# Top-2 experts on sorted rows: 23 padded tiles instead of all experts on all tokens

## The reference

```python
router_logits = xf @ router_w                      # (tokens, 8)
probs = softmax(router_logits)
rw, sel = top_k(probs, 2)
rw = rw / rw.sum(axis=-1, keepdims=True)
h = gelu(einsum('nc,ecf->enf', xf, w1e), approximate=False)   # 256 -> 512, each of 8 experts
y_all = einsum('enf,efc->nec', h, w2e)                        # 512 -> 256
y = (take_along_axis(y_all, sel) * rw[:, :, None]).sum(axis=1)
```

## Time and profile before

| | |
|---|---|
| median of 3 runs | 6225.56 us (6222.17 to 6227.89) |
| profiled execution, its time | 6224.38 us |
| profiled execution, its span | 6222.7 us |
| busy: PE, DVE, ACT, POOL | 4986.2, 4198.5, 2791.2, 1775.7 us |
| mean granted clock of TensorE | 0.88 |

### The profile page before, as it was taken

One profiled execution on the slowest core, in us unless ns is written; L12 is line 12 of the kernel. 1 busy time (PEld: TensorE's weight loads), 2 busy tenths in 40 slices (PEclk: granted clock), 3 DMA queues, 4 the chain that ended last, 5 costly groups with the idle time before them and its releaser, 6 DMA issues. The chain is left out here.

```text
span 6222.7 us, 84570 instructions
## 1 busy us (share of the span) xinstructions
PE 4986.2 (80%) x31689; PEld 3196.3 (51%) x31689; DVE 4198.5 (67%) x8611; ACT 2791.2 (45%) x5885; POOL 1775.7 (29%) x1429
## 2 busy tenths in 40 slices
PE   4444478888678988888678988889777998997789
PEld 2333345566335655666434654656534664665256
DVE  5999866777886856777786856668787755224511
ACT  2443315664354524656254633656344542553321
POOL 2565502333233401333232421334322430001000
PEclk7566689999789989999798998999888998998899
DMA  2000000000100110000201010000100010001000
GB/s 99 11 11 24 1 29 22 14 17 10 47 30 31 35 53 24 12 12 14 55 17 38 28 67 20 12 12 17 41 30 21 26 39 24 10 15 33 28 28 34
DMA packets 75086, 169.70 MB, mean 27 GB/s; under 512 B 15176, under 2 KB 36528, under 8 KB 71352
## 3 DMA queue, kind: packets, MB, share of 16 engines
q1 hardware_dynamic: 72632, 163.77, 8.3%
q10 hardware_dynamic: 2048, 0.53, 0.0%
HBM read 130.92 MB, written 26.26 MB: 25 GB/s over the span
## 5 line engine op out<-in xcount | busy, mean ns | idle before, releaser
L1373 DVE MAX8 vals<-work 128x8 f32<-128x128 f32 (+7 forms) x1536 | 1081.7, 745 | 0.6
L1718 POOL TENSOR_SCALAR keep<-ssb,vals 128x128 bf16<-128x128 f32 (+7 forms) x512 | 875.1, 1721 | 0.0
L1705 POOL TENSOR_TENSOR pool_step<-ones 128x2 f32<-128x2 f32 x256 | 49.5, 193 | 2536.4 <-DVE vals L1373 2536.2
L428 PE MATMUL ring<-ident,pr 128*128 128x128 f32 x2304 | 470.1, 323 | 360.4 <-POOL pr L1723 329.5
L1387 DVE MATCH_REPLACE8 work<-vals,work 128x128 f32<-128x128 f32 (+7 forms) x1024 | 751.5, 741 | 0.0
L535 PE MATMUL pA<-SC 128*128 128x512 f32 (+3 forms) x1536 | 626.7, 518 | 131.1 <-ACT SC L1116 109.6
L1723 POOL TENSOR_TENSOR pr<-keep,pr 128x128 f32<-128x128 bf16 (+7 forms) x512 | 647.2, 1285 | 0.0
L1055 ACT ACTIVATE prT<-ring 128x512 f32<-128x512 f32 (+1 forms) x768 | 379.4, 495 | 566.0 <-PE ring L428 564.8
L1502 DVE TENSOR_REDUCE nmax<-pA 128x1 f32<-128x1024 f32 (+7 forms) x512 | 382.7, 751 | 317.1 <-PE pA L536 306.0
L428 PEld LDWEIGHTS ring<-ident,pr 128*128 128x128 f32 x2304 | 326.4, 165 | 496.1 <-POOL pr L1723 355.3
L723 PE MATMUL pA<-hT,SC 128*128 128x512 f32 x1024 | 494.6, 606 | 0.0
(11 more groups left out here) (198 smaller groups left out, 8581.6 us busy)
## 6 DMA issues: line engine op xcount, KB each, us to landing
SC<-in_w SPq DMA_DIRECT2D x64, 512.0 KB, 4.4
parts<-SC SPq DMA_DIRECT2D x72, 256.0 KB, 2.4
SC<-in_wqkv SPq DMA_DIRECT2D x32, 384.0 KB, 2.9
stage<-parts SPq DMA_DIRECT2D x64, 192.0 KB
SC<-parts SPq DMA_DIRECT2D x24, 384.0 KB
stage<-parts SPq DMA_DIRECT2D x64, 128.0 KB
SC<-in_ffn_we SPq DMA_DIRECT2D x4, 2048.0 KB, 10.8
SC<-in_wqkv SPq DMA_DIRECT2D x8, 768.0 KB, 7.6
```

Source lines behind the costliest of these rows:

```text
L428: mm = pe.transpose(r[:, blk % 4 * P:blk % 4 * P + P], pr0[:, p % 2, blk * P:blk * P + P], ident[:, :])
L1373: m = v.max(vals0[:, y, i, 8 * n:8 * n + 8], src[:, lo:hi])
L1718: pool.tensor_scalar(keep0[:, lo:hi], ssb0[:, p % 2, lo:hi], vals0[:, p % 2, i, TOPK - 1:TOPK], None, ALU.is_ge).then_inc(s["k"], 1)
```

## The change

The expert stage is sorted by expert. For each batch:

1. DVE finds the two experts of each token and writes a one-hot of all 2048 choices into `hot`. PE counts with 17 small bf16 matmuls how many rows of the same expert come before each choice. DVE turns the counts into tiles of 128 rows per expert, padded, and into a slot for each choice (`slot_u`), and for each of 23 tiles the column at which its expert's weights begin (`expert_u`). PE reads these 23 numbers into registers.
2. POOL scatters the normalised rows (`xn5`) into HBM (`xs_dram`), in 16 indirect DMAs of 128 rows of 1 KB.
3. SP loads the rows back in chunks of 4 tiles. For each of the 23 tiles PE turns the rows, multiplies them with w1 (moving, 2 x 512 columns, from an address in a register), turns the Gelu's result and multiplies it with w2 (4 x 256 columns). ACT does every copy between. SP stores the output tile to `ys_dram`.
4. POOL waits for all stores and gathers 16 times 128 rows into `G`, and DVE weights and adds them, in four quarters.

All weights (8 MB) lie in SBUF at once, `wall`; SP loads four experts when flip's third group is through and four when flip's last values are done. The load of the tokens of batch b+2 moves behind the expert stage. Once, at the start, `xs_dram` is filled with 3 MB of x. The shares of the selection's ticks change with the stages.

```diff
+class Sparse:
+    TILES = (2 * N + E * (P - 1)) // P
+    CHUNK = 4
+    CHUNKS = -(-TILES // CHUNK)
+    WCOLS = KC * F + FC * D
+    def stored(self, b, j):
+        return b * len(range(j % 3, self.TILES, 3)) + j // 3
+SM = Sparse()
 class Pace:
-    STAGES = (("wide", 8 * 17, 0.47), ("prep", 12, 0.03), ("flip", 8 + 48, 0.21), ("moe", 64, 0.29))
+    STAGES = (("wide", 8 * 17, 0.49), ("prep", 12, 0.04), ("flip", 8 + 48, 0.22), ("route", 6, 0.06),
+              ("moe", 23, 0.13), ("collect", 6, 0.06))
...
-        expert_y = [pA[1][:, 512:512 + D], pV[:, 0:D]]
+        hidden_y = [pA[0][:, 0:512], pA[0][:, 512:N]]
         ident = sb("ident", [P, P])
         identm = sb("identm", [P, P], BF16)
         tri = sb("tri", [P, 2, P], BF16)
...
-        H = [cut(2048 * i, 2048).rearrange("p (f n) -> p f n", n=512) for i in range(2)]
-        w1_sb = [cut(4096 + 2048 * i, N).rearrange("p (k f) -> p k f", k=KC) for i in range(2)]
-        w2_sb = [cut(5120 + 2048 * i, N).rearrange("p (k f) -> p k f", k=FC) for i in range(2)]
+        wall = cut(0, E * SM.WCOLS)
+        xn5 = cut(16384, 2048).rearrange("p (t d) -> p t d", d=D)
+        xg = [cut(16384 + N * i, N).rearrange("p (t d) -> p t d", d=D) for i in range(2)]
+        xgT = cut(19968, 2 * KC * P).rearrange("p (i k n) -> p i k n", i=2, k=KC)
+        yb = [cut(lo, D) for lo in (20480, 20736, 18688)]
+        hb = hT[:, 0, :].rearrange("p (i n) -> p i n", i=2)
+        hbT = hT[:, 1, :].rearrange("p (i f n) -> p i f n", i=2, f=FC)
+        slot_f = hT[:, 0, 0:128].rearrange("p (i e) -> p i e", e=E)
+        slot_s = hT[:, 0, 128:144]
+        tile_c = hT[:, 0, 256:256 + SM.TILES * E].rearrange("p (j e) -> p j e", e=E)
+        tile_e = hT[:, 0, 512:512 + SM.TILES]
+        logit = hT[:, 0, 640:640 + NT * E].rearrange("p (t e) -> p t e", e=E)
+        G = cut(0, 2 * NT * D).rearrange("p (i d) -> p i d", d=D)
...
+        pe.wait_ge(m1["oh"], b + 1)
+        for k in range(17):
+            mm = pe.matmul(pV[:, P:P + 136], (ones_m if k else before_m)[:, :],
+                           hot[:, P - 8 * k:P - 8 * k + 136], start=(k == 0), stop=(k == 16))
+        mm.then_inc(m1["rk"], 1)
+        pe.wait_ge(m1["id"], b + 1)
+        first = [pe.value_load(expert_u[0:1, j:j + 1], min_val=0, max_val=(E - 1) * SM.WCOLS)
+                 for j in range(SM.TILES)]
+        for i in range(6):
+            at("route", i)
+        def turn_rows(j):
+            c = j // SM.CHUNK
+            if j % SM.CHUNK == 0:
+                pe.wait_ge(m1["xl%d" % (c % 2)], (b * 3 + c // 2 + 1) * 16)
+            r = bank(("mx", b, j))
             for k in range(KC):
...
+                mm = pe.transpose(r[:, k * P:k * P + P], xg[c % 2][:, j % SM.CHUNK, k * P:k * P + P],
+                                  ident[:, :])
+            mm.then_inc(s_rf, 1)
+        def hidden(j):
+            emptied(("mx", b, j))
+            if j >= 2:
+                pe.wait_ge(m1["ge"], b * SM.TILES + j - 1)
+            for k in range(KC):
+                mm = pe.matmul(hidden_y[j % 2], xgT[:, j % 2, k, :],
+                               wall[:, bass.ds(first[j] + k * F, F)], start=(k == 0), stop=(k == KC - 1))
             mm.then_inc(m1["h"], 1)
...
+        def turn(j):
+            pe.wait_ge(m1["ge"], b * SM.TILES + j + 1)
+            r = bank(("mh", b, j))
             for f in range(FC):
...
+                mm = pe.transpose(r[:, f * P:f * P + P], hb[:, j % 2, f * P:f * P + P], ident[:, :])
+            mm.then_inc(s_rf, 1)
+        def down(j):
+            emptied(("mh", b, j))
+            if j >= 2:
+                pe.wait_ge(m1["ye"], b * SM.TILES + j - 1)
+            for f in range(FC):
+                mm = pe.matmul(expert_y[j % 2], hbT[:, j % 2, f, :],
+                               wall[:, bass.ds(first[j] + KC * F + f * D, D)], start=(f == 0),
+                               stop=(f == FC - 1))
             mm.then_inc(m1["y"], 1)
...
+        turn_rows(0)
+        turn_rows(1)
+        pe.wait_ge(m1["w"], (b + 1) * 256)
+        hidden(0)
+        for j in range(SM.TILES):
+            if j + 2 < SM.TILES:
+                turn_rows(j + 2)
+            if j + 1 < SM.TILES:
+                hidden(j + 1)
+            turn(j)
+            if j:
+                down(j - 1)
+            at("moe", j)
+        down(SM.TILES - 1)
+        for i in range(6):
+            at("collect", i)
     def prelude(b):
...
+    for lo in range(0, SM.TILES * P, N):
+        n = min(N, SM.TILES * P - lo)
+        sp.dma_start(xs_dram[lo:lo + n], x[lo // N, 0:n]).then_inc(s_wld, 16)
...
+    def experts(those):
+        for e in those:
+            for dst, src in ((wall[:, e * SM.WCOLS:e * SM.WCOLS + KC * F], w1[e]),
+                             (wall[:, e * SM.WCOLS + KC * F:(e + 1) * SM.WCOLS], w2[e])):
+                sp.dma_start(dst, src).then_inc(m1["w"], 16)
     def moe(b, at):
...
+        def rows(c):
+            n = min(SM.CHUNK, SM.TILES - c * SM.CHUNK)
+            lo = c * SM.CHUNK * P
+            sp.dma_start(xg[c % 2][:, 0:n, :], xs_dram[lo:lo + n * P].rearrange("(t p) d -> p t d", p=P))\
+              .then_inc(m1["xl%d" % (c % 2)], 16)
+        for i in range(6):
+            at("route", i)
+        sp.wait_ge(m1["sc"], (b + 1) * 256)
+        rows(0)
+        rows(1)
+        for q in range(4):
+            if b:
+                sp.wait_ge(m1["ga%d" % q], b * 64)
+        for j in range(SM.TILES):
+            c = j // SM.CHUNK + 2
+            if j % SM.CHUNK == 0 and c < SM.CHUNKS:
+                filled(("mx", b, j + SM.CHUNK - 1))
+                rows(c)
+            sp.wait_ge(m1["ye"], b * SM.TILES + j + 1)
+            sp.dma_start(ys_dram[j * P:j * P + P], yb[j % 3]).then_inc(m1["ys%d" % (j % 3)], 16)
+            at("moe", j)
+        for i in range(6):
+            at("collect", i)
...
-        first_experts(b)
+        filled(("x", b, 2, 11, 3))
+        experts(range(2, 6))
+        sp.wait_ge(a2["pv"], (b + 1) * FL.GROUPS * FL.STEPS)
+        experts((0, 1, 6, 7))
         sp.wait_ge(a2["y"], b * NT + NT)
-        if b + 2 < B:
-            tokens(b + 2)
         if b + 1 < B:
             sp.dma_start(wo0, wo[0]).then_inc(t0["wo"], 16)
             group_weights(0)
         moe(b, at)
+        if b + 2 < B:
+            tokens(b + 2)
...
+        for i in range(6):
+            at("route", i)
+        def turned_rows(j):
+            r = filled(("mx", b, j))
+            if j >= 2:
+                act.wait_ge(m1["h"], b * SM.TILES + j - 1)
+            for k in range(KC):
+                m = act.activation(xgT[:, j % 2, k, :], r[:, k * P:k * P + P], ACT.Copy,
+                                   scale=lnw[:, 1, k:k + 1])
+            m.then_inc(s_re, 1)
+        def gelu(j):
+            act.wait_ge(m1["h"], b * SM.TILES + j + 1)
+            act.activation(hb[:, j % 2, :], hidden_y[j % 2], ACT.Gelu).then_inc(m1["ge"], 1)
+        def turned(j):
+            r = filled(("mh", b, j))
+            act.activation(hbT[:, j % 2, :, :].rearrange("p f n -> p (f n)"), r[:, :], ACT.Copy)\
+               .then_inc(s_re, 1)
+        def out_of_psum(j):
+            act.wait_ge(m1["y"], b * SM.TILES + j + 1)
+            if SM.stored(b, j):
+                act.wait_ge(m1["ys%d" % (j % 3)], SM.stored(b, j) * 16)
+            act.activation(yb[j % 3], expert_y[j % 2], ACT.Copy).then_inc(m1["ye"], 1)
+        turned_rows(0)
+        turned_rows(1)
+        gelu(0)
+        for j in range(SM.TILES):
+            if j + 2 < SM.TILES:
+                turned_rows(j + 2)
+            if j + 1 < SM.TILES:
+                gelu(j + 1)
+            turned(j)
+            if j:
+                out_of_psum(j - 1)
+            at("moe", j)
+        out_of_psum(SM.TILES - 1)
+        for i in range(6):
+            at("collect", i)
...
         ch.need(n)
...
+        ch.need(ch.mark(v.tensor_copy(ixf[:, :, :], ix8[:, :, 0:2])))
+        chosen = hot[:, P:2 * P].rearrange("p (i e) -> p i e", e=E)
+        v.tensor_tensor(chosen, iota8[:, :].unsqueeze(1).to_broadcast([P, 2 * NT, E]),
+                        ixf[:, :, :].rearrange("p t c -> p (t c)").unsqueeze(2).to_broadcast([P, 2 * NT, E]),
...
+        ch.mark(v.tensor_tensor(gsm[:, :, 4], gsm[:, :, 1], gsm[:, :, 3], ALU.mult))
+        v.wait_ge(m1["rk"], b + 1)
+        ch.need(ch.mark(v.tensor_scalar(count_u[:, 0, :], pV[:, 2 * P:2 * P + E], float(P - 1), None, ALU.add)))
+        ch.need(ch.mark(v.tensor_scalar(count_u[:, 1, :], count_u[:, 0, :], 7, None, ALU.logical_shift_right)))
+        ch.need(ch.mark(v.tensor_copy(heap[:, 0, 4:12], count_u[:, 1, :])))
+        ch.need(ch.mark(v.tensor_tensor(heap[:, 1, 4:12], heap[:, 0, 3:11], heap[:, 0, 2:10], ALU.add)))
+        ch.need(ch.mark(v.tensor_tensor(heap[:, 2, 4:12], heap[:, 1, 4:12], heap[:, 1, 2:10], ALU.add)))
+        ch.need(ch.mark(v.tensor_tensor(heap[:, 3, 4:12], heap[:, 2, 4:12], heap[:, 2, 0:8], ALU.add)))
+        before = heap[:, 3, 4:12].unsqueeze(1)
```

(53 more changed lines are left out.)

130 lines of the change are left out of this document (35 added, 95 removed).

## The result

The changed kernel takes 6111.7 us, median of four runs (6107.7 to 6116.8), against 6225.0 before. The ratio is 0.9818 with a 95% interval of 0.9801 to 0.9835: faster by 1.8%. The forecast was 6086, so 26 us too low, and inside its own range of 6022 to 6163.

The account below looks back on a forecast made before the run. PE bounds the expert stage, DVE the selection alone. Savings of 90 us (batches 0 to 2, net of moved ticks) and 59 (batch 3), plus 8 for weights and 2 at start: -139 from 6224.4, 6086 beside the median; range 6022 to 6163.

Parts of the forecast that it names:

- Chain: Route, ahead of the tiles: DVE's routing and PE's counting matmuls take 8 us until POOL may scatter.
- x: Scatter and gather: time one indirect DMA holds POOL, taken as 1.3 us; break-even 2.4.
- rival 1: Scatter and gather: POOL held until landing (x = 2.4, 6227 us) or, milder, by DVE (x = 2, 6176); chance 0.19, milder 0.06.
- Rival 2: Tiles: PE's sequencer binds through register addresses; 1.5 us more a tile costs 138 us, 2 gives 6270; chance 0.14.
- 0.25 us a tile: Tiles: allowance for PE's register addresses and 23 register loads, 6 us a batch, making the tiles 100 us.
- some 14 us in route for scores behind POOL: Route: sign expected, a DVE wait of this size for selection scores held up behind POOL's scatters.
- Batch 3: Last expert stage, no selection beside it: 127.6 + 32x = 169 us against 228.5 before, gain 59.
- Batches 0 to 2: Expert stages with selection beside them: 207 + 32x = 249 us against 293.4 before, gain 45 each.
- 29 us for 62 ticks: Tiles, batches 0 to 2: selection ticks lengthen PE's part by 0.47 us each, on top of 100 us.
- Both stay under 130: Tiles, batches 0 to 2: DVE's 95 us and ACT's 107 us of work fit within the stage's 130 us.
- 15 us a batch: Wide, flip and projections: cost of 19 ticks moved to earlier stages, 7 + 4 + 4 us.
- Weights beside flip's end: End of flip: 4 MB of weight loads delay ACT's small DMAs by 2 us a batch (bounds 0 and 3.3), 8 in all.

Follow-up runs that it names:

- e3: Changed kernel with POOL scattering only every second of the 16 row groups (half of the rows read are old): 6092.9 us, ratio 0.9788 to the kernel before.
- e2: Changed kernel with PE reading the 23 column numbers one or two tiles before use, after route's selection ticks: 6122.5 us, ratio 0.9832 to the kernel before.
- e5: Changed kernel with both half of the scatters left out and PE's register reads made late: 6084.4 us, ratio 0.9778 to the kernel before.
- e4: Changed kernel with ACT copying the hidden tile instead of taking the Gelu: 6075.2 us, ratio 0.9751 to the kernel before.
- e6: Changed kernel with the old selection shares in wide, prep and flip, and 19 ticks moved beside the tiles: 6184.3 us, ratio 0.9941 to the kernel before.
- e9: Changed kernel plus late weights, late register reads, split scatters and early sums, with 28 ticks moved from the tiles to wide: 6131.0 us, ratio 0.9854.
- e1: Changed kernel with SP holding the last four experts' weights until DVE's reciprocal of flip's last sums: 6096.9 us, ratio 0.9794 to the kernel before.

## Why the prediction was right, and where it was not

**Chain and x: right.** POOL starts 8 us behind the logits, and x is 1.27 us in the scatter, 1.25 in the gather. The scatters hold the path at this pitch where nothing else does, as e3 shows in batch 3 (1.27 us for each one left out); in batches 0 to 2 eight fewer alone gave 2.4 us, and no run takes gathers away. Neither dear form of rival 1 is seen. In batch 0 of the changed kernel DVE works beside the first four scatters and then waits; in e2 it works beside the first twelve. The pitch is 1.27 in both, and 1.27 with DVE idle in batch 3, so no wait of POOL for DVE shows, and the rule that the prediction quoted from the Trainium skill ("SBUF — State Buffer", section "SBUF: two separate sides") didn't come into play with these operations of DVE. The 2.3 us for such a DMA of the Trainium skill ("DMA: Bandwidth & Descriptors", section "Anatomy of one DMA — SWDGE (gpsimd) path") agree with the landings of 2.4 and 2.7 us and are no time that POOL is held: the next begins after 1.27. (With the prediction's own 128 us for each us of x, its sum for x = 2.3 is 6214, not 6216.)

**Rival 2, PE's sequencer in the tiles: no.** 23 rounds take 95.5 us in batch 3, 4.15 each, where 4.1 was the cost without any address work. The 0.25 us a tile that were added for it are 0.05 at most. But the same sequencer did cost elsewhere. The forecast had named the 23 register loads of a batch and priced them together with the addresses, as work hidden in the tiles; they stand ahead of route's selection, 0.69 us each, 15.9 in one piece. They hid behind POOL's wall, so they cost 0.3 us of route in this kernel (e2) and 8 once POOL was eased (e3 against e5). The wall of "some 14 us in route for scores behind POOL" was measured at 14.4 with another releaser: that number came true by luck.

**Batch 3: 160.5 against 169.** The tiles are 4.5 us shorter than forecast, for the reason above; the rest is in the landings and copies around them, each taken a little too long.

**Batches 0 to 2: 271.0 against 249.** Route is 65.8 against 62. Tiles are 142 against 130, the largest single error. The term that was too small is the 29 us for 62 ticks: 142 less the 95.5 of batch 3 is 46, and a tile term 4.5 too large hid a part of it. The step is "Both stay under 130", where the busy sums of DVE and ACT were compared with PE's time, found smaller, and the table loads then given no cost. e4 shows 15.4 us of table loads on the path though ACT was busy for 102 of 142, and 31 us for the ticks without them. The price of 0.47 a tick in the tiles was read from the old stage, in which PE had 288 us to cover 137 ticks; in the new one 62 ticks stand beside 95 us of PE, and e6 measures 20 us for 19 ticks more, 1.1 each. Collect is 63.3 against 57: the closing operations take 15.3 us, not 11, since a group of four takes 1.8 us and each quarter waits for itself, 0.48 an operation.

**Moved ticks: wrong in two of three places.** "15 us a batch" was made of 7 in wide, 4 in flip and 4 in projections. Measured with e6: -3 in wide, -4 in prep, +7 in flip, nothing in the projections: about zero. The step that failed is the price of a tick as the difference between a batch with all of its ticks and one with none, divided by their number. It is a mean over all ticks, and no single step has it: in wide the mean is 0.73 for 222 ticks, the next 9 cost about nothing and the 28 after them 1.6 each (e9).

**Weights beside flip's end: right mechanism, size wrong.** The term was 2 us a batch with bounds of 0 and 3.3. DVE's waits in e1 give 3.1 to 3.8 in batches 0 to 2, at the upper bound. With the 7.1 us of ticks from e6 that makes 10.5 of the 12.3 us by which flip grew there. In batch 3 it is 7.4 of 8.0: 4.5 at the end of flip and 3.0 for the first four experts beside the third group, which the term didn't have, since it looked only at flip's last DMAs. So the weights cost some 18 us and not 8.

**The sum.** Too good by 59 in the expert stages (3 x 22, less 8 in batch 3), too bad by 35 elsewhere. Of these 35, 48 are the moved ticks (forecast 45; measured -24 in wide and prep and +21 in flip); against them stand 16 that flip grew beyond its ticks (its growth of 45 less those 21 and less the 8 of the forecast; DVE's waits show 18 of these 24 for the weights, 6 stay open), and the rest of 3 is in the preludes and the start, where batch 0's first wide matmul came 1.0 us later and 2 were forecast. That leaves 24.
